# A selective scan on one core: the softplus's terms are added on PE, and Pool multiplies states with C in pairs over a ring of eight

## The chip, the cores and the metric

One NeuronCore of a Trainium2 chip runs the whole kernel in one launch. It has five engines that work side by side: PE (TensorE, matmuls), DVE (VectorE), ACT (ScalarE), POOL (GpSimd, called Pool here) and SP (SyncE, which here only issues transfers). The metric is the device time in microseconds. Lower is better. Three runs of the kernel before gave a median of 13330.74 us (13321.66 to 13340.04).

## The reference

The input is eight images of 96 channels by 64 x 64. Each goes through a group norm, a vision state-space block (in-projection, depthwise convolution, four-direction selective scan, gate, out-projection, and a convolutional side branch), then through an attention without softmax and a feed-forward layer with rounding to small float formats. The part that matters here is the scan, for each of 4 directions and 192 channels over 4096 positions, with 16 states per channel:

```python
delta = jax.nn.softplus(dts + dt_bias[None, :, :, None])
def step(h, inp):
    u_t, d_t, b_t, c_t = inp
    dA = jnp.exp(d_t[..., None] * A)
    h = dA * h + (d_t * u_t)[..., None] * b_t[:, :, None, :]
    y = jnp.einsum('bkdn,bkn->bkd', h, c_t)
    return (h, y)
```

## The kernel before, in words

A loop runs over the eight images. Per image there are a preparation (`prep_a`, `prep_b`), the scan (`scan()`), and a last part (`post`). The scan takes some 1280 us of the 1666 us of an image.

**Passes, chunks, states.** The scan has six passes T. Passes 0 to 2 go forward, 3 to 5 backward. T % 3 = 0 is the row order, T % 3 = 1 the column order for channels 0 to 127; T % 3 = 2 holds the remaining 64 channels, row order in the lower 64 partitions and column order in the upper. A pass has four chunks of 1024 positions, and a chunk has the states n = 0 to 15. So there are 24 chunks and 384 steps per image. The first chunk of a pass is "fresh": it takes no state from the chunk before.

**One step.** DVE's scan instruction (line 1220) makes `state[n]` from a decay and an input. ScalarE makes the decay as `exp(delta * a)` (line 1130). The input is `delta * u * B`. For ten of the states PE spreads the B row over 128 partitions into PSUM (`spread`, line 994) and DVE multiplies it by `du` (line 1207). For the six states in `POOLED = (2, 5, 7, 10, 13, 15)` a transfer spreads the row into `b_sb`, and Pool multiplies it by `du` (`times_b`, line 1250). After the scan ScalarE copies the last column to `carry` (line 1088), Pool multiplies the state in place by the C row that a transfer has spread over the partitions into `c_sb` (line 1261), and PE adds it into the PSUM tile `py` with an identity matmul (`add_up`, line 1017). ScalarE takes `py` out once per chunk (`take_y`, step `Y_AT` = 5).

**The softplus of the next chunk** is made during the present one, in PSUM tile `pc`. PE computes dt (`pre_dt`, line 1006, step 2). With x = dt + bias and e = exp(-|x|), the code forms relu(x) + ln(1 + e) and a correction of rounding, e - ((1 + e) - 1). ScalarE makes |x|, relu(x), e, 1 + e and the logarithm; DVE combines them in three passes over 128x1024 (`softplus_low`, `_high`, `_sum`, lines 1172, 1178, 1184) after the scans of states 7, 9 and 11 (`DT_AT`). Before the scan of state 15 DVE makes the next `du` = `pc` * u (line 1190), and ScalarE copies `pc` to `delta`.

**What sets the order.** Every engine runs a queue written out by hand and waits on semaphores at fixed places. `SUMS_AT` says behind which step PE adds which state: state m six steps after its scan. A spread waits until the scan two steps back is done, since two PSUM banks (`pb`) take turns. A scan waits until the state that held its slot in the ring `state` (`RING` = 7 slots) is summed. SP issues, for each step n, the load of C row n into `c_sb[n % 4]` once the product of state n - 4 is done (`weighted`), and the load of a B row `B_AHEAD` = 4 steps ahead of its step, once the product that last used the slot of `b_sb` is done. In passes T % 3 = 2 each load is two transfers, to 64 partitions each (line 946; line 942 otherwise). The transfers of one queue are started in order.

The weights `w_xp` of the projection that makes dt, B and C are built in the setup and stay in SBUF.

## Time and profile before

| | |
|---|---|
| median of three runs | 13330.74 us |
| span of the profiled execution | 13331.9 us |
| DVE busy | 11940.3 us (90%) |
| PE busy | 10547.0 us (79%) |
| Pool busy | 10383.8 us (78%) |
| ScalarE busy | 6832.0 us (51%) |
| mean granted PE clock | 0.902 |
| moved by DMA | 2404.29 MB, mean 180 GB/s |

The profiled execution is as long as the median of the timed runs. The busy shares are means over stages. The page's row of slices shows that DVE is at 9 tenths or more in the scan and at 7 between, so the scan has to be looked at by itself. A duration in a row reaches a little into the next instruction of its engine (0.05 to 0.1 us), so a cost per instruction is better read from start to start.

### The profile page before, as it was taken

The page shows a single profiled execution, that of the slowest core. Times are in us where ns is not written, and L with a number is a line of the kernel's source. Part 1 is how long each engine was busy: PE and PEld are TensorE (multiplying, and loading weights), DVE is VectorE, ACT ScalarE, POOL GpSimd, SP SyncE. Part 2 cuts the span into 40 slices and gives each one's busy share as a digit, 9 for nine tenths or more (in the row PEclk, how much of TensorE's full clock was granted, in tenths as well). Part 3 has the DMA queues.
Part 4 walks back from the last instruction along what each step waited for, and adds up shares of the span by engine and source line. Part 5 has one row for each costly group of instructions (what it writes and reads, how often), then busy time and mean ns, then how long its engine had stood idle before and what let it go on. Part 6 is the DMA issues. An engine that isn't in the chain of part 4 may idle for free. (4 is left out here: it accounts for less than half of the span.)

```text
span 13331.9 us, 95099 instructions
## 1 busy us (share of the span) xinstructions
PE 10547.0 (79%) x24646; PEld 4127.2 (31%) x24646; DVE 11940.3 (90%) x8647; ACT 6832.0 (51%) x10172; POOL 10383.8 (78%) x4597
## 2 busy tenths in 40 slices
PE   6777878778787787777878778777787777878778
PEld 2333323333233332333323333233332333323233
DVE  7999779997799978999789997799978999789997
ACT  4545555455555555555555555555555545555455
POOL 4999559994599945999459994599946999469994
PEclk8999988999889998999989999899998999988999
DMA  4676546764467644676446774467644677457774
GB/s 139 214 219 214 126 129 216 218 216 121 133 215 219 215 118 140 213 221 214 111 145 216 219 216 106 148 215 221 214 102 152 215 220 214 100 154 214 220 212 100
DMA packets 734798, 2404.29 MB, mean 180 GB/s; under 512 B 173200, under 2 KB 175248, under 8 KB 722768
## 3 DMA queue, kind: packets, MB, share of 16 engines
q1 hardware_dynamic: 734192, 2397.58, 61.1%
q8 instruction: 213, 3.49, 0.1%
q14 instruction: 393, 3.22, 0.1%
HBM read 2300.18 MB, written 67.11 MB: 178 GB/s over the span
## 5 line engine op out<-in xcount | busy, mean ns | idle before, releaser
L1261 POOL TENSOR_TENSOR state<-state,c_sb 128x1024 f32<-128x1024 f32 x3072 | 7182.5, 2358 | 464.2 <-ACT carry L1088 462.5
L1017 PE MATMUL ps<-state,wt 128*128 128x512 f32 x12288 | 6346.7, 659 | 164.0 <-ACT ya L1081 109.2
L1017 PEld LDWEIGHTS ps<-state,wt 128*128 128x128 f32 x12288 | 2558.9, 212 | 3061.6 <-issue 2490.5
L1220 DVE TENSOR_TENSOR_SCAN state<-decay,carry,ps 128x1024 f32<-128x1024 f32 x1440 | 3379.4, 2347 | 105.0 <-DVE ps L1207 38.9
L1088 ACT COPY carry<-state 128x1 f32<-128x1 f32 x3072 | 585.3, 191 | 4861.2 <-DVE state L1220 4852.1
L994 PE MATMUL ps<-parts,sel 114*128 114x512 bf16 (+1 forms) x3840 | 1288.7, 421 | 2083.4 <-DVE state L1220 2081.7
L1250 POOL TENSOR_TENSOR dbu<-b_sb,du 128x1024 f32<-128x1024 f32 x1152 | 2717.4, 2359 | 229.6 <-DVE du L1235 229.6
L1207 DVE TENSOR_TENSOR ps<-ps,du 128x1024 f32<-128x1024 f32 x1920 | 2323.4, 1210 | 0.9
L1130 ACT ACTIVATE decay<-delta,a_neg 128x1024 f32<-128x1024 f32 x1920 | 2194.9, 1144 | 6.9
L1220 DVE TENSOR_TENSOR_SCAN state<-ps,carry,dbu 128x1024 f32<-128x1024 f32 x864 | 2013.4, 2330 | 3.9 <-POOL dbu L1250 3.1
L994 PEld LDWEIGHTS ps<-parts,sel 114*128 114x128 bf16 (+1 forms) x3840 | 261.0, 100 | 3634.6 <-DVE state L1220 3361.7
L1130 ACT ACTIVATE ps<-delta,a_neg 128x1024 f32<-128x1024 f32 x1152 | 1278.4, 1110 | 0.0
L1220 DVE TENSOR_TENSOR_SCAN state<-decay,ps 128x1024 f32<-128x1024 f32 x480 | 1097.7, 2287 | 36.6 <-DVE ps L1207 12.9
L1577 POOL CAST h<-h16b 128x1536 fp8e5<-128x1536 f16 x64 | 116.2, 1815 | 896.0 <-DVE h16b L1702 896.0
L1220 DVE TENSOR_TENSOR_SCAN state<-ps,dbu 128x1024 f32<-128x1024 f32 x288 | 653.7, 2270 | 0.0
L1006 PE MATMUL ps<-parts,dt_w 114*128 114x512 bf16 (+1 forms) x1536 | 377.4, 389 | 98.4 <-ACT delta L1157 68.7
L1563 POOL TENSOR_TENSOR sqa<-sqa,sqr 64x512 f32<-64x512 f32 x64 | 100.5, 1570 | 393.8 <-ACT sqr L1471 393.8
L502 ACT ACTIVATE rs<-ps,wt 96x512 f32<-96x512 f32 (+1 forms) x320 | 218.7, 683 | 308.1 <-PE ps L487 171.9
L492 DVE TENSOR_TENSOR cen<-x,ps 96x512 f32<-96x512 f32 x192 | 130.6, 680 | 249.0 <-PE ps L487 248.3
L704 POOL TENSOR_SCALAR conv_acc<-pad_r,wt 128x512 f32<-128x512 f32 x8 | 12.6, 1569 | 387.2 <-POOLq L514 387.2
L487 PE MATMUL ps<-sq,wt 96*96 96x512 f32 x512 | 286.4, 643 | 21.7 <-ACT sq L497 20.6
L731 PE MATMUL ps<-pad_a,conv_diag 128*128 128x512 f32 x640 | 288.4, 613 | 11.3 <-PEq L514 11.3
(217 smaller groups left out, 10126.7 us busy)
## 6 DMA issues: line engine op xcount, KB each, us to landing
c_sb<-bc SPq DMA_DIRECT2D x2048, 512.0 KB, 4.3
c_sb<-bc SPq DMA_DIRECT2D x2048, 256.0 KB, 5.5
b_sb<-bc SPq DMA_DIRECT2D x768, 512.0 KB, 4.7
b_sb<-bc SPq DMA_DIRECT2D x768, 256.0 KB, 5.4
x_nat<-x SPq DMA_DIRECT2D x17, 1536.0 KB, 14.4
gates<-gate_a SPq DMA_DIRECT2D x8, 2048.0 KB, 6.8
x_tok<-x SPq DMA_DIRECT2D x288, 48.0 KB, 1.8
gn<-gn_t SPq DMA_DIRECT2D x8, 1536.0 KB, 7.3
```

What stands on the lines that cost most here:

```text
L487: pe.matmul(bank[0:C, :], col("ones_c", C), src[0:C, sl(j)], start=True, stop=True).then_inc(done, 1)
L502: act.activation(root[:, sl(j)], bank[0:p, :], ACT.Ln, bias=col("eps", p)).then_inc(logged, 1)
L731: mm = pe.matmul(conv_bank(i)[:, s * CH:(s + 1) * CH], conv_diag[:, t, :], pad_a[:, rows(j, t // 3), t % 3:t % 3 + W], start=(t == 0), sto ...
L994: mm = pe.matmul(bank[:, q * CH:(q + 1) * CH], sel[own, n, first:first + 128], part_cols(at, 2 * (T // 3), q, own), start=True, stop=True)
L1006: mm = pe.matmul(pc[:, q * CH:(q + 1) * CH], dt_w[own, p, w, :], part_cols(at, k, q, own), start=(i == 0 and p == 0), stop=(i == len(ways) ...
L1017: mm = pe.matmul(py[:, q * CH:(q + 1) * CH], col("ident"), state[:, slot(g, n), q * CH:(q + 1) * CH], start=(n == 0), stop=False)
L1088: act.copy(carry[:, n:n + 1], state[:, slot(g, n), last:last + 1]).then_inc(S["carried"], 1)
L1130: act.activation(pb[n % 2][:, :] if n in POOLED else decay[:, n % 2, :], delta[:, :], ACT.Exp, scale=a_neg[:, T, n:n + 1]).then_inc(S["dec ...
L1207: dve.tensor_tensor(pb[n % 2][:, :], pb[n % 2][:, :], du[:, :], ALU.mult)\
L1220: dve.tensor_tensor_scan(state[:, slot(g, n), way], rate, what, 0.0 if fresh else carry[:, n:n + 1], ALU.mult, ALU.add)\
L1250: pool.tensor_tensor(dbu[:, i % BRING, :], b_sb[:, i % BRING, :], du[:, :], ALU.mult)\
L1261: pool.tensor_tensor(state[:, slot(g, n), :], state[:, slot(g, n), :], c_sb[:, n % CRING, :], ALU.mult).then_inc(S["weighted"], 1)
```

## The change

Two things are changed, and some places are moved to fit.

**Softplus on PE.** The three DVE passes are gone. PE adds e and relu(x) into `pc` with identity matmuls (`sum_exp`, step 5), then the logarithm (`sum_ln`, step 10), then a rest term (`sum_rest`, step 13). ScalarE writes the logarithm over `relu_v` (step 7), then 1 + e over `zexp` (step 8, in step 5 before), and a new pass makes 1 - (1 + e) (step 9). Ahead of the first chunk of an image the same runs in one row.

**Pairs on Pool.** The ring has 8 slots. Pool multiplies two states at a time with two C rows (`times_c`), behind the odd step, once both are carried. SP frees and fills `c_sb` by pairs. The B row of state 2 is multiplied at the end of the chunk before (step 15, ahead of pair 14-15), and B loads are issued 5 steps ahead.

**Room.** The larger ring takes SBUF, so `w_xp` moves to a place that the scan overwrites. The setup stores it to DRAM, and each image loads it again behind `w_in`.

```diff
-RING = 7
+RING = 8
+PAIR = 2
-B_AHEAD = 4
+B_AHEAD = 5
-DT_AT = (7, 9, 11)
+TERMS_AT = (5, 10, 13)
-LN_AT = 9
+LN_AT = 7
...
+                    sp.dma_start(w_xp[:, :, :].rearrange("p i c -> p (i c)"), xp_dram).then_inc(S["w_in_loaded"], 16)
...
-                            pe.wait_ge(S["w_in_loaded"], 64)
+                            pe.wait_ge(S["w_in_loaded"], 80)
...
-                            sp.wait_ge(S["weighted"], g * NS + n - CRING + 1 + CREDIT)
+                            sp.wait_ge(S["weighted"], pair_of(g, n) - CRING // PAIR + 1 + CREDIT)
...
+                    def sum_exp(g):
+
+                        pe.wait_ge(S["dt_relu"], g + 1)
+                        pe.wait_ge(S["dt_exp"], g + 1)
+                        for q in range(2):
+                            half = slice(q * CH, (q + 1) * CH)
+                            pe.matmul(pc[:, half], col("ident"), zexp[:, half], start=True, stop=False)
+                            mm = pe.matmul(pc[:, half], col("ident"), relu_v[:, half], start=False, stop=False)
+                        mm.then_inc(S["dt_first"], 1)
...
-                        pe.wait_ge(S["weighted"], g * NS + n + 1 + CREDIT)
+                        pe.wait_ge(S["weighted"], pair_of(g, n) + 1 + CREDIT)
...
+                                if n == TERMS_AT[0]:
+                                    sum_exp(g + 1)
+                                if n == TERMS_AT[1]:
+                                    sum_ln(g + 1)
+                                if n == TERMS_AT[2]:
+                                    sum_rest(g + 1)
...
+                    def softplus_rest(g):
+
+                        act.wait_ge(S["dt_one"], g + 1)
+                        act.activation(zexp[:, :], zexp[:, :], ACT.Identity, bias=col("one"), scale=-1.0)\
+                           .then_inc(S["dt_rest"], 1)
...
-                            if n + 2 in POOLED:
+                            if n > 0 and n + 2 in POOLED:
                                 times_b(T, c, POOLED.index(n + 2))
...
+                            if n == NS - 1 and following:
+                                times_b(*following, 0)
+                            if n % PAIR == PAIR - 1:
+                                times_c(T, c, n - PAIR + 1)
+
+                    def times_c(T, c, n):
+
+                        g = c + T * NSC
+                        pool.wait_ge(S["carried"], g * NS + n + PAIR + CREDIT)
+                        for m in range(n, n + PAIR):
+                            pool.wait_ge(S[f"c_in_{m % CRING}"], c_landed(T, c, m))
+                        both = state[:, slot(g, n):slot(g, n) + PAIR, :]
+                        pool.tensor_tensor(both, both, c_sb[:, n % CRING:n % CRING + PAIR, :], ALU.mult)\
+                            .then_inc(S["weighted"], 1)
```

Pool's queue over the first eleven states of a chunk before. `state<-state,c_sb` is the product with C, `dbu<-b_sb,du` the product with a B row (here those of states 5, 7 and 10).

```order
L1261 TENSOR_TENSOR state<-state,c_sb 128x1024 [waits c_in_0,carried]
L1261 TENSOR_TENSOR state<-state,c_sb 128x1024 [waits c_in_1,carried]
L1261 TENSOR_TENSOR state<-state,c_sb 128x1024 [waits c_in_2,carried]
L1250 TENSOR_TENSOR dbu<-b_sb,du 128x1024 [waits scanned,b_in_1,du_ready]
L1261 TENSOR_TENSOR state<-state,c_sb 128x1024 [waits c_in_3,carried]
L1261 TENSOR_TENSOR state<-state,c_sb 128x1024 [waits c_in_0,carried]
L1250 TENSOR_TENSOR dbu<-b_sb,du 128x1024 [waits scanned,b_in_0,du_ready]
L1261 TENSOR_TENSOR state<-state,c_sb 128x1024 [waits c_in_1,carried]
L1261 TENSOR_TENSOR state<-state,c_sb 128x1024 [waits c_in_2,carried]
L1261 TENSOR_TENSOR state<-state,c_sb 128x1024 [waits c_in_3,carried]
L1250 TENSOR_TENSOR dbu<-b_sb,du 128x1024 [waits scanned,b_in_1,du_ready]
```

The same stretch of Pool's queue after the change, from pair 0-1 to the B row of state 10.

```order
L1297 TENSOR_TENSOR state<-state,c_sb 128x2048 [waits c_in_1,c_in_0,carried]
L1276 TENSOR_TENSOR dbu<-b_sb,du 128x1024 [waits scanned,b_in_1,du_ready]
L1297 TENSOR_TENSOR state<-state,c_sb 128x2048 [waits c_in_3,c_in_2,carried]
L1276 TENSOR_TENSOR dbu<-b_sb,du 128x1024 [waits scanned,b_in_0,du_ready]
L1297 TENSOR_TENSOR state<-state,c_sb 128x2048 [waits c_in_1,c_in_0,carried]
L1297 TENSOR_TENSOR state<-state,c_sb 128x2048 [waits c_in_3,c_in_2,carried]
L1276 TENSOR_TENSOR dbu<-b_sb,du 128x1024 [waits scanned,b_in_1,du_ready]
```

Before, Pool could begin with state 0 as soon as it was carried; now its first product with C stands behind the carry of state 1, and four pairs and two B products stand ahead of the product for state 10.

PE's queue around steps 4 to 6 of a chunk before: `ps<-parts,sel` is a spread, `ps<-state,wt` an addition of a state, `ps<-ua,d_diag` the last term of y of the chunk before.

```order
L994 MATMUL ps<-parts,sel 128x512 [waits scanned]
L994 MATMUL ps<-parts,sel 128x512
L1017 MATMUL ps<-state,wt 128x512 [waits weighted]
L1017 MATMUL ps<-state,wt 128x512
L1033 MATMUL ps<-ua,d_diag 128x512 x2
L994 MATMUL ps<-parts,sel 128x512 [waits scanned]
L994 MATMUL ps<-parts,sel 128x512
L1017 MATMUL ps<-state,wt 128x512 [waits weighted,y_taken]
```

The same place after the change (`zexp` holds e, `relu_v` holds relu(x)).

```order
L1069 MATMUL ps<-ua,d_diag 128x512 x2
L1028 MATMUL ps<-zexp,wt 128x512 [waits dt_exp,dt_relu]
L1029 MATMUL ps<-relu_v,wt 128x512
L1028 MATMUL ps<-zexp,wt 128x512
L1029 MATMUL ps<-relu_v,wt 128x512
L1005 MATMUL ps<-parts,sel 128x512 [waits scanned]
L1005 MATMUL ps<-parts,sel 128x512
L1053 MATMUL ps<-state,wt 128x512 [waits weighted,y_taken]
```

Two additions of softplus terms now stand ahead of the spread of state 6. Each matmul in this list is two in the trace, since f32 goes through PE in two parts.

## Rows read from the trace of the kernel before

**Rows 1.** Stretches: us; busy us of PE, PEld, DVE, ACT, POOL; clock, DMA share, GB/s.

```profile
415.00:631.00 216.00, 166.63 (x382) 65.49 (x382) 212.44 (x121) 108.88 (x156) 204.10 (x89) 0.92 0.63 213
631.00:843.00 212.00, 164.17 (x394) 65.42 (x394) 209.82 (x121) 107.26 (x156) 203.91 (x89) 0.93 0.92 219
...
1270.00:1484.00 214.00, 167.06 (x396) 66.94 (x396) 209.35 (x119) 105.70 (x155) 206.22 (x90) 0.93 0.88 213
```

**Rows 2.** The page, part 5: Pool's two products.

```profile
L1261 POOL TENSOR_TENSOR state<-state,c_sb 128x1024 f32<-128x1024 f32 x3072 | 7182.5, 2358 | 464.2 <-ACT carry L1088 462.5
...
L1250 POOL TENSOR_TENSOR dbu<-b_sb,du 128x1024 f32<-128x1024 f32 x1152 | 2717.4, 2359 | 229.6 <-DVE du L1235 229.6
```

**Rows 3.** Timeline of DVE, start us then us, pass 2, states 4 to 8.

```profile
700.61 1.21 DVE L1207 TENSOR_TENSOR ps<-ps,du 128x1024 f32<-128x1024 f32 x1
701.86 2.35 DVE L1220 TENSOR_TENSOR_SCAN state<-decay,carry,ps 128x1024 f32<-128x1024 f32 x1
704.12 2.32 DVE L1220 TENSOR_TENSOR_SCAN state<-ps,carry,dbu 128x1024 f32<-128x1024 f32 x1
706.36 1.21 DVE L1207 TENSOR_TENSOR ps<-ps,du 128x1024 f32<-128x1024 f32 x1
...
712.11 1.21 DVE L1172 SCALAR_TENSOR_TENSOR ps<-ps,zexp 128x1024 f32<-128x1024 f32 x1
713.22 1.22 DVE L1207 TENSOR_TENSOR ps<-ps,du 128x1024 f32<-128x1024 f32 x1
```

**Rows 4.** Timeline of DVE: `du` at two chunk ends of pass 0.

```profile
309.38 1.20 DVE L1190 TENSOR_TENSOR du<-ps,ua 128x1024 f32<-128x1024 f32 x1
...
362.41 1.20 DVE L1190 TENSOR_TENSOR du<-ps,ua 128x1024 f32<-128x1024 f32 x1
```

**Rows 5.** Line 1190, the product `du`: ns min/median/max.

```profile
L1190 DVE TENSOR_TENSOR du<-ps,ua x120: 1198/1907/1941, 256.4 to 12833.7; 128x1024 f32<-128x1024 f32 x120
```

**Rows 6.** Timeline of DVE, pass 1, state 6.

```profile
547.26 2.35 DVE L1220 TENSOR_TENSOR_SCAN state<-decay,carry,ps 128x1024 f32<-128x1024 f32 x1 [0.75 <-DVE ps L1207]
```

**Rows 7.** Timeline of ScalarE before it, states 5 and 6.

```profile
543.28 1.92 ACT L1081 COPY ya<-ps 128x1024 f32<-128x1024 f32 x1
544.99 1.12 ACT L1110 ACTIVATE ps<-zexp,wt 128x1024 f32<-128x1024 f32 x1
```

**Rows 8.** Groups by shape, Pool: smaller two-input products.

```profile
L715 POOL TENSOR_TENSOR conv_acc<-conv_acc,conv_tap 128x512 f32<-128x512 f32 x64 | 81.5, 1274 | 0.6
...
L530 POOL TENSOR_TENSOR conv_diag<-wt,conv_w 128x128 f32<-128x128 f32 x40 | 17.1, 462 | 0.3
```

**Rows 9.** Timeline of ScalarE, pass 2: the exponential of the softplus.

```profile
701.84 1.04 ACT L1104 ACTIVATE zexp<-zexp 128x1024 f32<-128x1024 f32 x1
```

**Rows 10.** Timeline of PE, pass 2.

```profile
704.26 0.61 PE L994 MATMUL ps<-parts,sel 114*128 114x512 bf16 x2 [2.97 <-DVE state L1220]
705.39 5.40 PE L1017 MATMUL ps<-state,wt 128*128 128x512 f32 x8 [0.53 <-ACT yr L1081]
...
732.35 3.60 PE L1017 MATMUL ps<-state,wt 128*128 128x512 f32 x8
```

**Rows 11.** Loads into `c_sb` in pass 2, issue to landing.

```profile
DMA to landing us min/median/max: 3.4/5.6/8.5
```

**Rows 12.** Timeline of ScalarE ahead of the first chunk.

```profile
199.31 1.06 ACT L1104 ACTIVATE zexp<-zexp 128x1024 f32<-128x1024 f32 x1
```

**Rows 13.** Timeline of DVE there: the product `du`.

```profile
205.34 1.22 DVE L1235 TENSOR_TENSOR du<-ps,ua 128x1024 f32<-128x1024 f32 x1
```

**Rows 14.** Timeline of DVE: the last scan.

```profile
1482.13 2.35 DVE L1220 TENSOR_TENSOR_SCAN state<-ps,carry,dbu 128x1024 f32<-128x1024 f32 x1
```

**Rows 15.** Timeline of PE: the last addition.

```profile
1489.06 1.98 PE L1017 MATMUL ps<-state,wt 128*128 128x512 f32 x4 [0.31 <-POOL state L1261]
```

**Rows 16.** Timeline of SP: weights for the next image.

```profile
1716.23 2.92 SPq L519 DMA_DIRECT2D w_in_sb<-phase_weights  x4
```

**Rows 17.** Timeline of PE: their first use.

```profile
1730.23 1.10 PE L611 MATMUL ps<-cen,w_in_sb 96*128 96x512 f32 x2
```

More of the change, by code:

```diff
@@ L109, in build @@
 def build(nc, x, weights, phase_weights, setup_weights, out, gate_dram, gn_dram):
+    xp_dram = nc.dram_tensor("xp", (128, 5 * 128), F32, kind="Internal").ap()
     bc_dram = nc.dram_tensor("bc", (NDIR, 2, NS, L), F32, kind="Internal").ap()
@@ L138, in build @@
     carry = put("carry", [128, NS], F32)
-    w_xp = put("w_xp", [128, 5, 128], F32)
     gn_scale = put("gn_scale", [C, GROUPS], F32)
@@ L191, in build @@
     gn_work = at("gn_work", [C, 352], F32, C0 + 512 + 23552)
+    w_xp = at("w_xp", [128, 5, 128], F32, C0 + 512 + 25088)
     conv_diag = at("conv_diag", [128, PE_TAPS, 128], F32, C0 + 512 + 20480)
@@ L275, in build @@
         ur_in xp_mm xp_hi xp_out xp_rest xp_mid xp_low parts_zero bc_stored parts_in pre_mm dt_abs
-        dt_relu dt_exp dt_one dt_ln dt_low dt_high delta_sum delta_ready du_ready b_mm decayed dbu_ready
+        dt_relu dt_exp dt_first dt_ln dt_one dt_rest delta_sum delta_ready du_ready b_mm decayed dbu_ready
         dbu_pooled scanned carried weighted summed y_summed y_taken c_in_0 c_in_1 c_in_2 c_in_3 b_in_0
@@ L375, in _ @@
                 sp.wait_ge(S["w_loaded"], 80 + 16 * GROUPS)
+                sp.wait_ge(S["setup_dve"], 7)
+                sp.dma_start(xp_dram, w_xp[:, :, :].rearrange("p i c -> p (i c)")).then_inc(S["w_loaded"], 16)
+                sp.wait_ge(S["w_loaded"], 96 + 16 * GROUPS)
             @block.scalar
@@ L433, in _ @@
                                                          (DT0 + RANK * g, 2 * g + order, 6 * NS, RANK)):
-                                nc.vector.tensor_copy(w_xp[lo_p:hi_p, i, to:to + count],
-                                                      from_[lo_p:hi_p, st, src, first:first + count])
+                                last = nc.vector.tensor_copy(w_xp[lo_p:hi_p, i, to:to + count],
+                                                             from_[lo_p:hi_p, st, src, first:first + count])
+                last.then_inc(S["setup_dve"], 1)
             @block.tensor
@@ L924, in slot, with pair_of @@
                 return (g * NS + n) % RING
+            def pair_of(g, n):
+                return (g * NS + n) // PAIR
             def c_landed(T, c, n):
@@ L1009, in pre_dt, with sum_ln, sum_rest @@
                         mm.then_inc(S["pre_mm"], 1)
+                    def sum_exp(g):
[6 more added lines that the diff above has]
+                        mm.then_inc(S["dt_first"], 1)
+                    def sum_ln(g):
+                        pe.wait_ge(S["dt_ln"], g + 1)
+                        for q in range(2):
+                            half = slice(q * CH, (q + 1) * CH)
+                            pe.matmul(pc[:, half], col("ident"), relu_v[:, half], start=False, stop=False)
+                    def sum_rest(g):
+                        pe.wait_ge(S["dt_rest"], g + 1)
+                        for q in range(2):
+                            half = slice(q * CH, (q + 1) * CH)
+                            mm = pe.matmul(pc[:, half], col("ident"), zexp[:, half], start=False, stop=True)
+                        mm.then_inc(S["delta_sum"], 1)
                     def add_up(g, n):
@@ L1056, in steps @@
                                 pre_dt(following[0], next_at)
+                            if following:
+                                if n == TERMS_AT[0]:
[4 more added lines that the diff above has]
+                                    sum_rest(g + 1)
                     pre_dt(0, 0)
+                    sum_exp(0)
+                    sum_ln(0)
+                    sum_rest(0)
                     each_chunk(steps)
@@ L1143, in steps @@
                                     softplus_exp(g + 1)
-                                if n == PRE_AT + 3:
-                                    softplus_one(g + 1)
                                 if n == LN_AT:
                                     softplus_ln(g + 1)
+                                if n == LN_AT + 1:
+                                    softplus_one(g + 1)
+                                if n == LN_AT + 2:
+                                    softplus_rest(g + 1)
                                 if n == NS - 1:
@@ L1153, in _ @@
                     softplus_exp(0)
+                    softplus_ln(0)
                     softplus_one(0)
-                    softplus_ln(0)
+                    softplus_rest(0)
                     act.wait_ge(S["du_ready"], 1)
@@ L1255, in steps @@
                         for n in range(NS):
-                            if n + 2 in POOLED:
+                            if n > 0 and n + 2 in POOLED:
                                 times_b(T, c, POOLED.index(n + 2))
-                            pool.wait_ge(S["carried"], g * NS + n + 1 + CREDIT)
-                            pool.wait_ge(S[f"c_in_{n % CRING}"], c_landed(T, c, n))
-                            pool.tensor_tensor(state[:, slot(g, n), :], state[:, slot(g, n), :], c_sb[:, n % CRING, :],
-                                               ALU.mult).then_inc(S["weighted"], 1)
+                            if n == NS - 1 and following:
[10 more added lines that the diff above has]
+                            .then_inc(S["weighted"], 1)
+                    times_b(0, 0, 0)
                     each_chunk(steps)
```

31 lines of the change are left out of this document (4 added, 27 removed).

## The prediction

> **What bounds the kernel now.** I read the stretches first [rows 1]: one row for each of three of the six passes of the scan in the first image. The reader is to see DVE busy 209 to 212 of every 212 to 216 us, Pool 204 to 206, PE 164 to 167, ScalarE 105 to 109. DVE is the bound and Pool is 4% behind it, so what DVE gives up, Pool can take over after little. The last two columns come next: in pass 1 DMA moves 213 GB/s at a share of 0.63, in pass 2 219 GB/s at 0.92. Passes 2 and 5 load each row in two halves of 64 partitions, and that costs share: at full share the first kind would move 213/0.63 = 338 GB/s, the second 219/0.92 = 238. A row of `c_sb` or `b_sb` (128x1024 f32, 524,288 bytes) takes 1.55 us of it in passes 0, 1, 3, 4 and 2.20 us in passes 2 and 5, 1.10 per half.
>
> Then the DVE timeline [rows 3], start to start: a product with `du` 1.25 us (700.61 to 701.86), a scan 2.26, a scan of a pooled state 2.24, a softplus pass 1.11. A chunk of 16 states is 10 x (1.25 + 2.26) + 6 x 2.24 + 3 x 1.11 + 1.12 for `du` = 53.0 us, and two chunk ends stand 53.03 apart [rows 4]. In passes 1 and 4 `du` reads by columns and takes 0.7 longer [rows 5], and scan 6 comes 0.75 late [rows 6], since ScalarE does a 1.92 us copy of y and a softplus pass between two decays [rows 7]: 54.4. In pass 5 the y copy is in two parts and I count 54.0 (the stretch of 214 us holds four chunks and the last has no softplus).
>
> **DVE's part.** The three passes of lines 1172, 1178, 1184 go from each chunk: 53.0 - 3.3 = 49.7 us. ScalarE's pass of step 5 moves to steps 8 and 9, where no y copy stands beside it, so the 0.75 goes too; passes 1 and 4 keep 0.7 for `du`: 50.4. If nothing else came late, that would be it.
>
> **Pool's part.** One product takes 2358 ns [rows 2]; 512 elements take 1274 and 128 take 462 [rows 8]. The slope is 2.117 ns per element, the rest 0.19 us. A pair of 2048 is then 4.53 us, 4.48 start to start, against 2 x 2.31. Bounds: 4.62 if nothing fixed is saved, 4.43 if all 0.19 are; I take 4.48. Pool's work per chunk is 8 x 4.48 + 6 x 2.31 = 49.7, as much as DVE's. The GPSIMD Engine Reference of the Trainium skill (section Elementwise) has 4497 ns measured for an f32 `tensor_tensor` of 2048; by it Pool's chunk would be some 0.2 us shorter. Its key points also speak of contention with DVE instructions that read two SBUF inputs; by that the slope above, partly from a stage in which DVE does other work, would be too low, but 128, 512 and 1024 lie on one line.
>
> But a pair can start only when its second state is scanned, and Pool takes its queue in order. Count from the start of `du`. Scan 1 ends at 1.12 + 2.24 + 2 x 3.51 + 0.09 = 10.5, its carry is copied by 10.8, and only then can Pool start pair 0-1, then B5, pair 2-3, B7, 4-5, 6-7, B10: 4 x 4.48 + 3 x 2.31 = 24.9, ready at 35.7. DVE would want B10 for scan 10 at 34.65. So DVE stands 1.05 us per chunk: period 50.7 (passes 0, 3) and 51.4 (1, 4). Pool is idle 1.0 of it, waiting for scan 1. The other pooled states come in time (B5 17.6 for 19.6, B7 24.4 for 25.4).
>
> **PE's part.** Four more additions per chunk of four matmuls each: 1.72 us each at the full clock (eight take 3.60 [rows 10]), 6.9 us on an engine with 48 us free in each pass of 212. The place matters: the first two stand ahead of the spread of state 6. The exponential they wait for ends at 702.9 [rows 9]; two additions are 3.45, the spread 0.61, so it lands at 706.9 where DVE wants it at 706.36 [rows 3]: 0.6 late. This stall lies inside the 1.05 that Pool causes, as it delays only scans ahead of scan 10. It costs nothing more.
>
> The granted clock matters here. Rows 10 show eight matmuls at 5.40 us after PE had stood 2.97 and 0.53, and 3.60 elsewhere. I walk PE's queue through a new chunk and find no gap over 1.9 us. TensorE: Matmul & The Clock Gate of the Trainium skill (section The HAM clock gate) says that activity releases the throttle; by it the added matmuls raise the clock, and it would lower no term above.
>
> **The loads.** A `c_sb` pair is free when its product ends, so three rows (C, B, C) are issued at once where one was issued before: after 12-13, after 14-15, after 4-5. The next user of that pair starts one pair and one B later: 6.8 us. The first row lands in about 3.4 us at the least [rows 11], for the first half alone. Passes 0, 1, 3, 4: 3.4 + 2 x 1.55 = 6.5, in time. Passes 2 and 5: six halves, 3.4 + 5 x 1.10 = 8.9, with 0.1 to 0.3 for the issue 9.1: 2.3 late. I follow it once around: the loads after 12-13 and after 4-5 each cost Pool 2.3; the one after 14-15 is hidden by the first delay. Pool has 49.7 of work, so the period is 49.7 + 4.6 = 54.3, against 53.0 in pass 2 and 54.0 in pass 5. The longest landing of one half in pass 2 is 8.5 us [rows 11]; by that a group lands at 11.5 and the period is 59.
>
> **Ends of each image.** Ahead of the first chunk the softplus has nothing beside it. Before: from the exponential's end (200.4) [rows 12] to `du` (205.3) [rows 13] 5.0 us. After: two additions, ln, one, rest, one addition: 3.45 + 3.25 + 1.72 = 8.4 at the full clock, 14.9 at half (6.9 + 4.6 + 3.4): +3.4 to +9.9, I take +6. At the end pair 14-15 is a single product: before, the last addition starts at 1489.06 [rows 15], 4.6 after the last scan's end [rows 14]; after, Pool is 2 us later and two additions follow: +3.7. The weights `w_xp` now come by DMA: issued behind the four of 1716 to 1719, landed about 1723, and in_proj starts at 1730.23 [rows 16, 17]: 0. If that cover were gone, 2 us. The store in the setup costs some 2 us once.
>
> **The sum**, against the span of 13331.9 (median 13330.74, so the same within 0.01%). Per image: passes 0 and 3: 8 x -2.3 = -18.4; passes 1 and 4: 8 x -3.0 = -24.0; pass 2: +3.9 (three chunks; the first is still free of the delay); pass 5: +4.7 (the last chunk had no softplus to lose, hence most of it); fresh chunks, whose scans are 0.06 shorter but wait for Pool all the same, and the first chunk: +3.2. That is -30.6; the ends +9.7. Net -20.9, x 8 = -167: **13165 us**, 1.2% faster.
>
> **The rivals.**
> (A) The loads don't bite: groups land within 6.8 + 1.0. Against it the 338 and 238 GB/s; for it that before, in-order loads in pass 2 never stop Pool. Passes 2 and 5 go to 50.7: -3.6 x 7 chunks x 8 = -200: 12965.
> (B) DVE bounds all: besides (A) the pair starts sooner or is shorter and B10 comes in time: another 1.05 x 24 x 8 = -200: 12765. The queue order speaks against it.
> (C) Slower: the two additions ahead of the spread of state 6 run at the half clock. Then they take 6.9, the spread is late by 4.4, not 0.6, and every chunk is 49.7 + 4.4 = 54.1: 16 x 3.1 x 8 = +400 on the forecast: 13560. It decides from where the mean period passes 52.0, an addition pair of 5.2 us, midway between the two clocks. For it the 5.40 in rows 10, against it the gap ahead, 1.8 instead of 3.0 us.
> (D) Slower: groups land as late as the longest half says. 59 in passes 2 and 5: +4.7 x 7 x 8 = +260: 13430.
> (E) The pair saves nothing on Pool (4.62): B10 0.6 later, 24 x 8 x 0.6 = +115: 13280.
>
> **Chances.** Forecast 49%, A 22%, B 7%, C 7%, D 7%, E 8%. The range of 13165 alone is 13080 to 13260. The range on record reaches to A below and past E and half of D above: 12930 to 13370. A measurement of this kernel tells 0.2% (27 us) from nothing: faster 80% (forecast, A, B, a quarter of E), same 6% (the rest of E), slower 14% (C, D).
>
> **What would show it.** DVE: no rows of the three passes; an idle of about 1 us ahead of scan 10 that the Pool product of `dbu` ends; 0.6 us ahead of the product of state 6. Pool: 1536 products of 2048 at 4.53 us, and in passes 2 and 5 idle time ended by DMA, some 4.6 us per chunk, none in the others. Chunk periods of 50.7, 51.4 and 54.3. PE's clock above 0.95 in the scan. Wrong: Pool's waits on DMA absent (A), DVE waiting for PE by 4 us at state 6 (C), a pair over 4.6 us (E).

## The result and the profile after

The changed kernel takes 13355.8 us (median of 20 runs, 13340.4 to 13366.0), the kernel before 13329.6 us in its 20 runs (13312.7 to 13340.0). The ratio is 1.0018, with a 95% interval of 1.0011 to 1.0025. So the change costs 0.2% where 1.2% less was forecast: 13165 us, 191 us too low, though 13355.8 lies inside the range. The profiled execution spans 13355.1 us.

The page of the kernel after, busy time per engine and two product groups of Pool (columns: busy us and mean ns; idle ahead and what ended it):

```profile
PE 11314.8 (85%) x27718; PEld 4479.1 (34%) x27718; DVE 11352.2 (85%) x8071; ACT 7039.3 (53%) x10364; POOL 10164.9 (76%) x3061
...
L1297 POOL TENSOR_TENSOR state<-state,c_sb 128x2048 f32<-128x2048 f32 x1536 | 6954.6, 4531 | 621.6 <-DMA c_sb<-bc 415.7
...
L1276 POOL TENSOR_TENSOR dbu<-b_sb,du 128x1024 f32<-128x1024 f32 x1152 | 2714.8, 2357 | 281.2 <-DVE du L1261 281.2
```

DVE did lose 588 us of work and Pool 219 us, and the pair costs 4531 ns, as forecast. But the time didn't follow: 415.7 us of new Pool idle time end with a load into `c_sb`, where in [rows 2] ScalarE's `carry` was the releaser. Five rows of the table of waits follow (us in total, times, longest):

```profile
POOL state L1297 <- DMA c_sb<-bc: 415.7, 344, 3.9
...
DVE state L1256 <- POOL dbu L1276: 325.5, 317, 2.8
...
POOL state L1297 <- ACT carry L1134: 168.9, 112, 5.9
...
DVE ps L1243 <- PE ps L1005: 152.2, 174, 3.9
...
DVE du L1261 <- PE ps L1044: 135.7, 8, 17.7
```

Of these waits only Pool's for `carry` had any weight before, with 462.5 us [rows 2]; DVE's scans waited 3.1 us for Pool, and there was none of the other three. Passes 0, 1, 2 and 5 of the first image, the columns of [rows 1], and then 20 us behind the scan:

```profile
217.00:427.00 210.00, 181.52 (x422) 66.15 (x420) 198.10 (x109) 111.55 (x161) 195.22 (x56) 0.93 0.67 216
427.00:632.00 205.00, 179.28 (x448) 71.61 (x447) 199.29 (x109) 113.05 (x160) 199.06 (x57) 1.00 0.68 224
632.00:852.00 220.00, 182.95 (x457) 72.46 (x455) 197.67 (x108) 111.20 (x160) 197.73 (x56) 0.98 0.87 210
1264.00:1481.00 217.00, 176.19 (x431) 69.30 (x429) 195.45 (x106) 105.60 (x154) 195.94 (x56) 0.98 0.86 209
1500.00:1520.00 20.00, 15.54 (x25) 5.36 (x24) 10.10 (x13) 7.02 (x12) 4.85 (x3) 0.76 1.04 257
```

DVE and Pool have 195 to 199 us of work in each pass. Pass 1 takes 205 us, nearly that; pass 2 takes 220 for the same work. By passes, from first scan to first scan (pass 5 to the end of its last scan), mean over the eight images, as counted from the rows of both traces (the last column is the forecast's term):

| pass | before | after | change | forecast |
|---|---|---|---|---|
| 0 | 212.3 | 209.0 | -3.3 | -9.2 |
| 1 | 215.5 | 206.4 | -9.1 | -12.0 |
| 2 | 211.9 | 221.1 | +9.2 | +3.9 |
| 3 | 211.9 | 205.3 | -6.6 | -9.2 |
| 4 | 215.5 | 205.7 | -9.8 | -12.0 |
| 5 | 209.0 | 218.2 | +9.2 | +4.7 |
| fresh and first chunks | | | in the passes | +3.2 |
| between two scans | 383.5 | 396.9 | +13.4 | +9.7 |
| image | | | +3.0 | -20.9 |

Eight times +3.0 is 24 us, the 23.2 by which the span grew. Of the 23.9 us per image between forecast and measurement, 9.8 lie in passes 2 and 5, 5.9 in pass 0, 4.5 in passes 1, 3 and 4 (7.7 less the 3.2 of the fresh chunks), and 3.7 between the scans.

Pool over one chunk of pass 2, from pair 0-1 to pair 8-9 (start us, us; in brackets the idle time ahead and its end):

```profile
805.79 4.52 POOL L1297 TENSOR_TENSOR state<-state,c_sb 128x2048 f32<-128x2048 f32 x1 [2.83 <-DMA c_sb<-bc]
810.28 2.35 POOL L1276 TENSOR_TENSOR dbu<-b_sb,du 128x1024 f32<-128x1024 f32 x1
812.63 4.53 POOL L1297 TENSOR_TENSOR state<-state,c_sb 128x2048 f32<-128x2048 f32 x1
...
824.12 4.53 POOL L1297 TENSOR_TENSOR state<-state,c_sb 128x2048 f32<-128x2048 f32 x1 [0.16 <-DMA c_sb<-bc]
828.59 2.36 POOL L1276 TENSOR_TENSOR dbu<-b_sb,du 128x1024 f32<-128x1024 f32 x1
834.11 4.51 POOL L1297 TENSOR_TENSOR state<-state,c_sb 128x2048 f32<-128x2048 f32 x1 [3.16 <-DMA c_sb<-bc]
```

And DVE in the same chunk, where the delay arrives:

```profile
812.67 2.35 DVE L1256 TENSOR_TENSOR_SCAN state<-ps,carry,dbu 128x1024 f32<-128x1024 f32 x1 [1.10 <-POOL dbu L1276]
...
819.50 2.35 DVE L1256 TENSOR_TENSOR_SCAN state<-ps,carry,dbu 128x1024 f32<-128x1024 f32 x1 [0.97 <-POOL dbu L1276]
...
830.98 2.35 DVE L1256 TENSOR_TENSOR_SCAN state<-ps,carry,dbu 128x1024 f32<-128x1024 f32 x1 [2.13 <-POOL dbu L1276]
...
840.97 2.35 DVE L1256 TENSOR_TENSOR_SCAN state<-ps,carry,dbu 128x1024 f32<-128x1024 f32 x1 [0.62 <-POOL dbu L1276]
...
847.85 1.23 DVE L1226 TENSOR_TENSOR du<-ps,ua 128x1024 f32<-128x1024 f32 x1 [1.03 <-POOL dbu L1276]
```

Two loads per chunk are late, ahead of pairs 0-1 and 8-9, by 2.83 and 3.16 us here where 2.3 was forecast. Behind each late pair the B products end late, and the scans that need them wait. Behind pair 0-1 DVE waits 1.10, 0.97 and 2.13 us ahead of scans 5, 7 and 10. Behind pair 8-9 it waits 0.62 ahead of scan 13 and 1.03 ahead of `du`, which stands until Pool's last B product, that of state 15, is done.

In pass 0 the wait is another. PE in the third chunk, a stretch of it (us; busy us of PE, PEld, DVE, ACT, POOL; clock, DMA share, GB/s), and DVE's product of state 6 behind it:

```profile
328.55 0.60 PE L1005 MATMUL ps<-parts,sel 48*128 48x512 bf16 x2 [1.38 <-DVE state L1256]
329.08 3.06 PE L1053 MATMUL ps<-state,wt 128*128 128x512 f32 x4
332.07 1.03 PE L1005 MATMUL ps<-parts,sel 48*128 48x512 bf16 x2
333.04 3.78 PE L1053 MATMUL ps<-state,wt 128*128 128x512 f32 x4
336.61 1.92 PE L1069 MATMUL ps<-ua,d_diag 128*128 128x512 f32 x4
```

```profile
330.00:332.00 2.00, 2.00 (x3) 0.34 (x1) 1.97 (x3) 1.23 (x3) 2.00 (x1) 0.50 1.01 373
```

```profile
342.54 1.23 DVE L1243 TENSOR_TENSOR ps<-ps,du 128x1024 f32<-128x1024 f32 x1 [2.55 <-PE ps L1005]
```

Four matmuls take 3.78 us and then 1.92: PE ran at 1.2 GHz for about 7 us (clock 0.50), after gaps of 0.93, 0.85 and 1.38, shorter than the 2.97 of [rows 10]. Everything behind them is late: the softplus additions, themselves at the full clock again, and the spread of state 6, for which DVE waits 2.55. That is not quite rival C, where the additions themselves are slow. Those come in the first chunk of pass 0, where no state of an earlier chunk is there to be added and PE stands for 4.99 and then 4.68 us:

```profile
231.37 2.05 PE L1028 MATMUL ps<-zexp,wt 128*128 128x512 f32 x2 [4.68 <-ACT zexp L1150]
```

```profile
237.06 1.23 DVE L1243 TENSOR_TENSOR ps<-ps,du 128x1024 f32<-128x1024 f32 x1 [2.38 <-PE ps L1005]
```

Each image has such a wait in its first chunk (gaps of 4.4 to 5.6 and 4.7 us ahead), and a fall of the clock some 112 us into pass 0.

Last, the ends. Ahead of the first chunk:

```profile
203.02 2.05 PE L1028 MATMUL ps<-zexp,wt 128*128 128x512 f32 x2 [3.24 <-ACT zexp L1150]
...
209.89 1.98 PE L1037 MATMUL ps<-relu_v,wt 128*128 128x512 f32 x4 [1.24 <-ACT relu_v L1155]
212.11 1.98 PE L1044 MATMUL ps<-zexp,wt 128*128 128x512 f32 x4 [0.23 <-ACT zexp L1164]
```

From the exponential's end (202.9) to `du` (214.13) it is 11.3 us, 6.3 more than the 5.0 of [rows 12, 13]; 6 was forecast. Behind the last scan (1478.99 + 2.35) Pool's last pair starts at 1484.11 and the first copy of y at 1494.12, and DVE's first instruction of `post` waits 19.66 us where it waited 13.50:

```profile
1484.11 4.50 POOL L1297 TENSOR_TENSOR state<-state,c_sb 128x2048 f32<-128x2048 f32 x1 [0.69 <-DMA c_sb<-bc]
...
1501.00 0.69 DVE L1621 TENSOR_TENSOR ya<-ya,ps 128x512 f32<-128x512 f32 x1 [19.66 <-PE ps L1346]
```

From the last scan's end to that copy it is 12.8 us, and was 8.3: the tail costs 4.5 (3.7 forecast). The rest of the +13.4 is 2.6 us. Of it 1.7 lies between the copy and DVE's first instruction (6.9 us for 5.2), where PE's six groups of matmuls take 4.35 us for 2.65; PE is slower in `post`, with a granted clock of 0.76 from 1500 to 1520, and 0.91 in the same stretch before. The last 0.9 was not located.

### The profile page after: what moved, and what is told of

The parts are those of the page before. It is cut to its first block and busy times, and to the rows that moved or that the text cites. A ratio compares the mean times of both kernels' runs of the same rounds, so it can differ in the third digit from the quotient of the medians.

```text
span 13355.1 us, 97605 instructions
## 1 busy us (share of the span) xinstructions
PE 11314.8 (85%) x27718; PEld 4479.1 (34%) x27718; DVE 11352.2 (85%) x8071; ACT 7039.3 (53%) x10364; POOL 10164.9 (76%) x3061
## 5 line engine op out<-in xcount | busy, mean ns | idle before, releaser
L1297 POOL TENSOR_TENSOR state<-state,c_sb 128x2048 f32<-128x2048 f32 x1536 | 6954.6, 4531 | 621.6 <-DMA c_sb<-bc 415.7
L1053 PE MATMUL ps<-state,wt 128*128 128x512 f32 x12288 | 5824.0, 611 | 135.0 <-POOL state L1297 119.7
L1256 DVE TENSOR_TENSOR_SCAN state<-decay,carry,ps 128x1024 f32<-128x1024 f32 x1440 | 3379.5, 2347 | 51.4
L1053 PEld LDWEIGHTS ps<-state,wt 128*128 128x128 f32 x12288 | 2330.5, 194 | 2726.2 <-issue 2103.6
L1243 DVE TENSOR_TENSOR ps<-ps,du 128x1024 f32<-128x1024 f32 x1920 | 2322.8, 1210 | 154.3 <-PE ps L1005 152.2
L1005 PE MATMUL ps<-parts,sel 114*128 114x512 bf16 (+1 forms) x3840 | 1177.0, 389 | 1208.9 <-DVE state L1256 1205.9
L1028 PE MATMUL ps<-zexp,wt 128*128 128x512 f32 x768 | 426.7, 638 | 202.3 <-ACT zexp L1150 201.0
L1029 PE MATMUL ps<-relu_v,wt 128*128 128x512 f32 x768 | 406.6, 612 | 0.0
L1037 PE MATMUL ps<-relu_v,wt 128*128 128x512 f32 x768 | 361.8, 593 | 9.9 <-ACT relu_v L1155 9.9
L1044 PE MATMUL ps<-zexp,wt 128*128 128x512 f32 x768 | 361.8, 593 | 1.9 <-ACT zexp L1164 1.9
## 6 DMA issues: line engine op xcount, KB each, us to landing
x_nat<-x SPq DMA_DIRECT2D x17, 1536.0 KB, 14.1
```

Of the source, the lines that this page charges most:

```text
L1005: mm = pe.matmul(bank[:, q * CH:(q + 1) * CH], sel[own, n, first:first + 128], part_cols(at, 2 * (T // 3), q, own), start=True, stop=True)
L1028: pe.matmul(pc[:, half], col("ident"), zexp[:, half], start=True, stop=False)
L1029: mm = pe.matmul(pc[:, half], col("ident"), relu_v[:, half], start=False, stop=False)
L1037: pe.matmul(pc[:, half], col("ident"), relu_v[:, half], start=False, stop=False)
L1053: mm = pe.matmul(py[:, q * CH:(q + 1) * CH], col("ident"), state[:, slot(g, n), q * CH:(q + 1) * CH], start=(n == 0), stop=False)
L1243: dve.tensor_tensor(pb[n % 2][:, :], pb[n % 2][:, :], du[:, :], ALU.mult)\
```

## The experiments

All ratios are to the kernel before in the same session. E3, E4, E6 and E8 start from the changed kernel.

**E1 and E2: the two halves of the change, each alone.** E1 is the kernel before with the softplus's terms on PE, Pool's products single and the ring at seven; E2 is the changed kernel with the softplus on DVE as before.

```diff
 # E1, to the kernel before (E2 takes the rest of the change and leaves this out)
-DT_AT = (7, 9, 11)
+TERMS_AT = (5, 10, 13)
-LN_AT = 9
+LN_AT = 7
...
 # PAIR, RING = 8, times_c in pairs, B_AHEAD = 5, w_xp: not taken over
```

> The kernel before with the softplus on PE and ScalarE alone; Pool, ring, loads and w_xp as before. Theory (what eats the gain is the triple of loads, C, B, C, that pairs make SP issue at once, in passes 2 and 5): here rows are issued one by one, so Pool never waits for DMA and passes 2 and 5 take 204 to 208 us like the others. Pool's 22 products of 2.31 us are 50.8 us per chunk and become the bound: scan stage 1238 us per image (1276 before, 1266 after), ahead of the first chunk +6. Total about 13080. Rival (the transfers of passes 2 and 5 cannot be supplied faster however they are issued, 48 us of transfer per chunk): passes 2 and 5 stay at 212 and more, total 13150 or more. Rival (the additions on PE hold up the spreads and eat the gain): DVE waits for spreads 3 us per pass and more, total above 13200.

> The changed kernel with the softplus on DVE and ScalarE as in the kernel before; pairs, ring of eight, loads and w_xp as changed. Theory of the triples: passes 2 and 5 at 55 us per chunk as in the changed kernel (pass 2 about 220 us, pass 5 about 218), the others as before (212 and 215.5); the end of each image 4 to 7 us longer. Total about 13530, 1.5% slower than before. Rival (Pool simply has too little to spare once DVE is faster): here DVE is as slow as before, all passes as before, total 13330 to 13390.

Measured: E1 12960.6 us, ratio 0.9726 (0.971 to 0.9742). E2 13514.6 us, ratio 1.014 (1.0123 to 1.0157). E1 beats even its theory by 120 us; E2 meets its own, with 219.5 us in pass 2 and 215.8 in pass 5. The softplus's move is worth 2.7%, and the pairs cost all of it: they cost 1.4% on the old softplus and, by the two medians, 395 us on the new one. "The pairs" are here all that came with them: the ring of eight, the loads by pairs, the B product moved to the chunk before, and `w_xp`. E1's stretches (the second chunk of pass 0, then pass 1) show what bounds it:

```profile
260.00:311.00 51.00, 47.17 (x112) 17.10 (x112) 49.64 (x28) 27.86 (x41) 51.00 (x23) 0.97 0.67 227
419.00:623.00 204.00, 180.44 (x448) 72.37 (x447) 199.13 (x110) 113.23 (x161) 203.56 (x89) 0.99 0.66 225
```

Pool is busy all 51.00 us of the chunk. With single products its work is 22 x 2.31 = 50.8 us, and this chunk takes 50.9 (mean of the eight images; E1's chunks from the second of pass 1 on take 50.5 to 51.7). The forecast had 50.7 for the chunk with pairs: so by its own prices the pairs could bring 0.1 us.

**E3 and E6: is it the triple of loads?** E3 moves B's loads behind the second C of a pair, E6 loads a whole row in one transfer in passes 2 and 5 too (both halves of the partitions then get the same row, so that those passes use other B and C values; the time is what is asked).

```diff
 # E3
-B_AHEAD = 5
+B_LOAD_AT = {1: 5, 3: 7, 5: 10, 9: 13, 11: 15, 13: 2}
...
# E6
-                        if T % 3 < 2:
-                            sp.dma_start(dst, ...broadcast_to([128, SC]))
-                        else:
-                            for h in range(2):
-                                sp.dma_start(dst[DR * h:DR * h + DR, :], ...broadcast_to([DR, SC]))
+                        sp.dma_start(dst, ...broadcast_to([128, SC])).then_inc(S[landed], 16)
```

> The changed kernel, SP's B load moved behind the second C load of a pair (steps 1, 3, 5, 9, 11, 13); everything else the same. Theory of the triples: the pair then waits for four halves and not six, 3.4 + 3 x 1.1 = 6.7 us against the 6.8 it has, so the DMA waits of Pool in passes 2 and 5 (16 to 19 us per pass) fall to under 3, both passes go to 205 us, total about 13115. Rival (supply: 22 rows of 2.2 us per chunk leave DMA no slack, the wait only moves): passes 2 and 5 stay above 213 us, total above 13250.

> The changed kernel, but in passes 2 and 5 each row is loaded by one transfer to 128 partitions instead of two to 64 (the upper 64 partitions get the row of the lower ones, so the column order of the third part of the channels is computed from wrong rows). Theory (six halves at 1.1 us each are late, three rows at 1.55 are not): passes 2 and 5 fall from 220 and 218 us to 204 to 206, Pool's wait for DMA in them from 19 and 16 us to 5, total 13355 - 30 x 8 = 13115. Rival (pairs wait whatever the transfers cost, since they are issued late): the passes stay above 213, total above 13250.

Measured: E3 13102.0 us, ratio 0.9836 (0.982 to 0.9853); E6 13071.2 us, ratio 0.9806 (0.979 to 0.9823). Both totals meet their theories (13115). In the parts E3 falls short: passes 2 and 5 take 208.5 and 206.4 us for 205, and Pool still waits 8.3 us for loads in each where under 3 was expected. E6 has 205.7 and 201.3 us. Pass 2 in E3 and in E6 (same columns):

```profile
629.00:836.00 207.00, 179.40 (x458) 72.72 (x456) 196.62 (x108) 111.09 (x160) 197.82 (x57) 0.99 0.94 223
```

```profile
629.00:836.00 207.00, 180.59 (x465) 73.45 (x464) 199.35 (x110) 112.08 (x161) 201.58 (x58) 1.00 0.69 226
```

E3 moves the same bytes at the same high share of 0.94, in another order, and pass 2 falls from 221.1 to 208.5 us. So what most of the delay came from was the place in the queue, not the total. E6 shows what the half transfers cost: 226 GB/s at a share of 0.69 against 223 at 0.94. It also halves the number of issues in these passes, and SP takes 0.60 us over each half and 0.43 over a whole row (medians), so E6 alone doesn't tell the transfer's cost from the issue's. What E3 leaves against E1, 141 us, lies for the most part in passes 2 and 5 again (5.1 and 5.0 us per image).

**E7: does the stall at state 6 lie inside the one at state 10?** The forecast said that 0.6 us of waiting for PE cost nothing more. E7 is E3 with dt's matmuls and ScalarE's first three passes of the softplus one step earlier.

```diff
-PRE_AT = 2
+PRE_AT = 1
```

> e3 (B loads behind the pair of C) with dt and the first three ScalarE passes of the softplus one step earlier (PRE_AT 1), so that PE can add the first two terms right behind the last term of y and be done before the spread of state 6. As predicted (the stall at state 6 lies inside the one ahead of state 10, which Pool's queue sets from the carry of state 1): DVE's waits for PE go (3 us per pass), its waits for Pool's product of state 10 come instead, total within 30 us of 13102. Rival (in series): 0.75 us per chunk and more in pass 0, 20 us per image, total about 12940.

Measured: 13106.0 us, ratio 0.983 (0.9813 to 0.9846), the same as E3. Two rows of waits of E3, and two of E7:

```profile
DVE ps L1243 <- PE ps L1005: 191.9, 200, 4.0
...
DVE state L1256 <- POOL dbu L1276: 134.3, 144, 2.9
```

```profile
DVE state L1256 <- POOL dbu L1276: 287.1, 191, 4.9
...
DVE ps L1243 <- PE ps L1005: 58.3, 98, 2.1
```

134 us of waiting for PE go, and 153 us of waiting for Pool come. The claim holds: a stall was moved, not removed. Passes 1, 3 and 4 keep their times to 0.2 us. Pass 0, where the waits for PE were longest, falls by 1.6 us (208.7 to 207.1): its chunks 1 to 3 take 50.8, 50.8 and 51.5 us for 52.4, 51.3 and 51.8, but its first takes 54.1 for 53.2. Pass 2 gives 1.4 back.

**E4: the softplus's first additions behind the spread of state 6.**

```diff
-TERMS_AT = (5, 10, 13)
+TERMS_AT = (6, 10, 13)
-LN_AT = 7
+LN_AT = 8
```

> The changed kernel with the first two softplus additions one step later (behind the spread and the addition of step 6) and ScalarE's logarithm at step 8. As predicted, the stall of DVE ahead of state 6 lies inside the one that Pool's queue causes ahead of state 10: the DVE waits for PE (3 us per pass) go, those for Pool grow by as much, total within 30 us of the changed kernel (13330 to 13360). Rival (the stall stands in series, above all where PE runs at its half clock, 7.8 us in pass 0): 14 us per image less, total about 13240.

Measured: 13515.4 us, ratio 1.0139 (1.0122 to 1.0156), 160 us slower than the changed kernel. Both expectations missed. PE in pass 1, two stretches of it (columns as above), and the product of DVE that waits:

```profile
544.33 3.59 PE L1067 MATMUL ps<-ya,wt 128*128 128x512 f32 x4
549.17 0.61 PE L1005 MATMUL ps<-parts,sel 114*128 114x512 bf16 x2 [1.26 <-DVE state L1256]
551.22 3.78 PE L1053 MATMUL ps<-state,wt 128*128 128x512 f32 x4 [1.44 <-ACT ya L1127]
554.80 1.92 PE L1028 MATMUL ps<-zexp,wt 128*128 128x512 f32 x2
...
560.90 0.60 PE L1005 MATMUL ps<-parts,sel 114*128 114x512 bf16 x2
```

```profile
544.00:546.00 2.00, 2.00 (x4) 0.48 (x3) 2.00 (x2) 0.74 (x3) 2.00 (x2) 1.00 0.63 227
...
550.00:552.00 2.00, 0.78 (x1) 0.50 (x2) 2.00 (x2) 2.00 (x2) 2.00 (x2) 0.50 0.48 186
```

```profile
561.53 1.23 DVE L1243 TENSOR_TENSOR ps<-ps,du 128x1024 f32<-128x1024 f32 x1 [4.43 <-PE ps L1005]
```

The first addition of step 6 waits until ScalarE has copied y. In the changed kernel the softplus's additions filled PE's time ahead of it; behind it they and the next spread queue up. PE stands for 1.26 and then for 1.44 us, and its clock falls as the second begins: it is 1.00 up to 549 and 0.50 from 550 to 556. So the addition at 551.22 takes 3.78 us in place of 1.88, and the softplus's first two matmuls 1.92 in place of 1.10. The 3.59 us of the line 1067 are no sign of the clock. It reads `ya` by columns and takes as long at 1.00, in the changed kernel too:

```profile
539.67 3.59 PE L1067 MATMUL ps<-ya,wt 128*128 128x512 f32 x4
```

DVE waits for PE 499.8 us in all, 152.2 in the changed kernel; the mean clock is 0.930, against 0.956. So the place that the change chose for the additions is right, and rival C's mechanism is real one step further on.

**E10: the pairs alone, with E3's order of loads.** E2 with `B_LOAD_AT` as in E3.

> The pairs without the softplus's move, as in the run of 13515 us, and B's loads behind the second C instead of between the two. Theory (the pairs' only price was the late triple of loads): passes 2 and 5 fall from 220 and 215.5 us to about 213 and 210, where VectorE's own 53.0 us a chunk bounds; with the later start and end of each image that leaves 13375 to 13400 us, no better than the kernel before, because Pool's time was not what bound it. Rival (the pairs cost something beside the loads, such as a shared port or dbu coming late for the products on VectorE): the time stays at 13480 us or more.

Measured: 13404.0 us, ratio 1.0064 (1.0048 to 1.0081), 4 us past the theory's upper edge and 76 us below the rival's bound. Its passes 1 to 5 take 215.4, 211.9, 211.9, 215.4 and 209.6 us, those of the kernel before to 0.6 us, though Pool has 4 us less to do in each: before, DVE bounded and Pool's time was free. What is left of the loss is pass 0 (215.3 against 212.3) and the ends (388.2 against 383.5).

**E5: the first chunk's softplus on DVE.** E1, with the softplus ahead of an image's first chunk in three DVE passes as before.

```diff
-                    sum_exp(0)
-                    sum_ln(0)
-                    sum_rest(0)
...
+                    dve.scalar_tensor_tensor(pc[:, :], pc[:, :], 1.0, zexp[:, :], ALU.subtract, ALU.subtract)
+                    dve.tensor_tensor(pc[:, :], relu_v[:, :], pc[:, :], ALU.subtract)
+                    dve.tensor_tensor(pc[:, :], zexp[:, :], pc[:, :], ALU.add)
```

> e1 (softplus on PE, Pool as before) with the first chunk's softplus of each image on DVE as in the kernel before, where nothing runs beside it. Theory: the way from the exponential to the first scan is 14.4 to 15.9 us with PE and was 8.5 with DVE, and the granted clock of the first pass's first chunks is not touched otherwise: 6.3 x 8 = 50 us less than e1's 12961, about 12910. Rival (the time comes back, since PE is colder in the first chunk and its additions ahead of the spread of state 6 take longer): under 15 us less.

Measured: 12912.2 us, ratio 0.9684 (0.9668 to 0.97), 48 us under E1 by the two medians, 6.0 us per image and so the price of the prologue in the forecast. By the traces it is 6.7 us between two scans; the two runs come from different sessions.

**E8 and E9: can the pairs be made to pay?** E8 adds to the changed kernel E3's idea, E7's earlier dt, E5's prologue, the last pair as two products, and B5's product ahead of pair 0-1. E9 is E8 with single products in passes 2 and 5.

```diff
 # E8
+B_LOAD_AT = {3: 7, 5: 10, 9: 13, 11: 15, 13: 2, 15: 5}
+PRE_AT = 1
...
+                            if n == 1:
+                                times_b(T, c, 1)
...
# E9
+            def paired(g):
+                return g // NSC % 3 < 2
...
+                            if paired(g):
+                                if n % PAIR == PAIR - 1:
+                                    times_c(T, c, n - PAIR + 1, PAIR)
+                            else:
+                                times_c(T, c, n, 1)
```

> Pairs and softplus on PE with the four mends: B loads behind the pair of C; the product for state 5 ahead of pair 0-1 on Pool (its load at step 15), so that it is out of the chain from state 1 to state 10; dt one step earlier; first chunk's softplus on DVE; the last pair of an image as two products. Theory: the chunk is bound by DVE and Pool at 49.7 to 49.9 us each (50.5 with the product by columns), passes 199 to 203 us, scan stage 1205, between images 384 as before: total about 12750, below e1. Rival (supply of passes 2 and 5, 48 us of transfers per chunk and more with gaps, decides there): these passes stay at 206 and more, total 12830 or more.

> Pool takes its steps in pairs only in passes 0, 1, 3 and 4, where B comes for nothing but the first states, and one at a time in passes 2 and 5. The rest is that of the kernel with the first chunk's softplus on VectorE, B5's product ahead of the first pair and the last steps as single products. Theory (a pair is worth its 4.5 us a chunk only where no fresh B loads have to pass beside C's): passes 0, 1, 3, 4 stay at 206, 202.8, 200.4, 203 us as with all pairs, passes 2 and 5 fall from 209.9 and 207.0 to the 203.4 and 201.4 that the single products showed with the softplus on TensorE. Scan stage about 1217 us, between images about 384.5: 12865 us, below the 12912 of the version without pairs. Rival (passes 2 and 5 are held by where the loads stand, not by the pairs): they stay at 206 or more, and the kernel takes 12920 us or more.

Measured: E8 12999.1 us, ratio 0.9753 (0.9736 to 0.9769); E9 12893.2 us, ratio 0.9676 (0.966 to 0.9692). E8 misses its theory by 250 us: passes 2 and 5 stay at 209.9 and 207.0, as its rival said. E9 lies between its two expectations: pass 2 falls to 205.0, pass 5 to 203.2, with the same rows loaded. So it is the pairs and the places that go with them, not the amount to be loaded, that hold these passes in E8. E9's `du` at two chunk ends of pass 0:

```profile
261.55 1.20 DVE L1234 TENSOR_TENSOR du<-ps,ua 128x1024 f32<-128x1024 f32 x1
311.40 1.20 DVE L1234 TENSOR_TENSOR du<-ps,ua 128x1024 f32<-128x1024 f32 x1
```

49.85 us: there the pairs do what they can, and DVE's own 49.7 bound. But 1 us per chunk in the later chunks of passes 0 and 3, less what E9 pays elsewhere (its first chunk of pass 0 takes 54.7 us where E5's takes 52.0, that of pass 2 52.3 where E5's takes 50.8), leaves E9 level with E5: their intervals overlap. E5 is the simpler kernel at the same time, 3.2% under the kernel before.

## Why the prediction was wrong, step by step

**DVE's part: right.** Chunks of passes 1 and 4 take 51.6 and 51.4 us in the mean (51.4 forecast), the first three of pass 3 50.9, 50.8 and 50.9 (50.7). E9 shows the floor of 49.7 behind them. No row of the three passes is left in the scan.

**Pool's part: the price right, the conclusion missing.** A pair is 4531 ns. The GPSIMD Engine Reference of the Trainium skill (section Elementwise) has 4497 for an f32 `tensor_tensor` of 2048; the trace is 0.8% over that. The stall ahead of scan 10 is there: 0.60, 0.67 and 0.39 us in the mean in passes 1, 3 and 4, behind 0.75 at state 6, together 1.15 to 1.4 where 1.05 was forecast. But the step never put the other sum beside its own: without pairs Pool's chunk is 22 x 2.31 = 50.8 us, against 50.7 with them, since what the pair saves is lost by waiting for the second state. "Pool can take over after little" hid that. By these prices the pairs as built had 0.1 us per chunk to bring, and what serves them could only cost. This is the step whose repair would have changed the advice, though not the number.

**The loads: the mechanism right, the size wrong; this is the largest term that failed.** The triple after 12-13 and after 4-5 was late in each chunk of passes 2 and 5, as the forecast said, and E3 and E6 show it to be the cause: 254 us and 285 us go when it goes. The sum had +8.6 us per image for these passes, and +18.4 were measured. Three sizes were off. Pool waits 2.8 and 2.6 us ahead of pair 0-1 (pass 2, pass 5) and 2.4 and 2.5 ahead of pair 8-9, for 2.3 each (loads end 2.5 and 1.9 of them in pass 2, 2.5 and 1.2 in pass 5, a carry or a scan the rest); the two late pairs of the chunk shown put the landing at 9.6 and 10.0 us for 9.1. Ahead of pair 6-7, whose C rows are issued behind B10, it waits another 0.4 and 0.2, which the step has not. That makes 5.6 and 5.5 us on top of 49.7, and the chunks behind the first take 55.0 to 56.1 us for 54.3. And the first chunk of pass 2, which the sum left as it was (52.8), takes 54.9: its own pair 0-1 waits 2.75 us. The load after 14-15 is hidden, as forecast (pair 2-3 waits 0.1 us at most in the mean); so is a fourth triple that the step overlooked, C10, B15, C11 after 6-7. The rest of this step, that passes 0, 1, 3 and 4 have no wait for loads, is wrong in a small way: Pool waits there too, 4.0, 4.4, 4.3 and 3.7 us per pass.

The loads alone don't turn the sign. With +18.4 in its place the sum would still have been -11.1 us per image, 0.7% faster. The other 14.1 are 5.9 in pass 0, 4.5 in passes 1, 3 and 4, and 3.7 at the ends, and all fell on the same side.

**PE's part: right for most chunks, wrong for pass 0.** The wait of 0.6 us at state 6 came as 0.75 and lies inside Pool's stall (E7). The mean clock rose from 0.902 to 0.956. But the step "no gap over 1.9 us" fails twice. It isn't so: the first chunk of pass 0 has gaps of 4.99 and 4.68 us, and passes 2 and 5 have gaps of 2.0 to 2.9. And where it is so, it was taken for "no half clock": in the third chunk of pass 0 gaps of 0.85 to 1.38 us stood ahead of the slow stretch. DVE waited 7.6 us for PE in the first image's pass 0, and the pass gained 3.3 in place of 9.2. E7 takes these waits away and brings the later chunks of pass 0 near the forecast's 50.7; what holds its first chunk is not settled, and nor is the share of the 5.9 us that each has. TensorE: Matmul & The Clock Gate of the Trainium skill (section The HAM clock gate) was read as if more work meant a full clock at all times; by it the mean should rise, and it did, but E4 with the same matmuls in another order lost half of that gain (0.930). How short a gap is safe, no run here settles.

**Ends: +9.7 forecast, +13.4 measured.** Prologue 6.3 for 6, tail 4.5 for 3.7, `w_xp` 0 as forecast (PE never waits for it). The step has no term for `post`, which takes 2.6 us more; 1.7 of them stand beside a slower PE. That PE's wait for the last pair (3.07 us) brings the lower clock is likely and not shown. The step's bound at the half clock also let ScalarE's three passes grow from 3.25 to 4.6 us with no reason given; they took 3.4 (208.69 to 212.06).

**The rivals.** A (loads don't bite) and E (a pair of 4.62) are out. B's period of 49.7 came only in E8 and E9, in passes 0 and 3. C came in the first chunk of pass 0, and half-clock matmuls ahead of the additions in single chunks after it. D had the right place and sign, but 59 us was too much: 55.2 is nearer to the forecast's 54.3. The measured time lies inside the range only by the part of D that the range took in, and D's period is not what came.

## What to carry to other kernels

When a change relieves two engines, add up each engine's work per period with each half of the change alone. Here 22 x 2.31 us said that the pairs bought 0.1 us, and what they needed cost more: a larger burst of loads (254 us, E3) and a later tail (4.5 us per image). What the later first product cost was not tried alone. When operations are merged, what frees and fills their buffers comes in bursts; look at which transfer in the burst is wanted first, and put it first: E3 gained 1.9% by moving loads a place back in their queue. And a stall that lies inside a later one on the same engine gave nothing when it was removed alone (E7).
